# Six graph-attention layers on one core: exponentials of layer 0 in other slots, layer 1's projection tied to ScalarE's copies, and a new order for the last items

## The chip, the core and the metric

The kernel runs on one core of a Trainium2 chip. TensorE (PE, with its weight loads shown as PEld), VectorE (DVE), ScalarE (ACT), GpSimd (POOL) and SyncE (SP, which issues the DMAs) each work through a queue of their own in order, and wait for each other only through semaphores. The metric is device microseconds of one execution.

## The reference, cut to what matters

128 graphs of 128 nodes with 256 features pass through six attention layers. Layer 0 has eight heads, layer 1 one head of width 256, layers 2 to 5 one head of width 128.

```
layer 0:     q,k,v = x@W + b ; attn = softmax(mask(q k^T / sqrt(32))) per head
             x = layernorm(x + (attn@v)@Wo + bo)
layer 1:     attn = softmax(mask((x@Wq)(x@Wk)^T / 16)) ; x = layernorm(x + attn@(x@Wv)@Wo + bo)
layers 2..5: attn = softmax(mask((x@Wq+bq)(x@Wk+bk)^T / sqrt(128)))
             x = layernorm(x + (attn@x)@Wc^T)
```

## The kernel before, in words

**Groups and slots.** Two graphs make a group; there are 64 groups. The program is a list of slots, and every engine walks the same list, each with its own fixed order of work inside a slot. Five slots make a period. In a period the slots project, in order of time, layer 2, layer 1, layer 5, layer 4 and layer 3, each for another group (`item(i)` gives layer and group of slot i). An item is projected in its slot i, its softmax is done in slot i+1, and its context, residual and normalisation in slot i+2. Below, "the layer-2 slot" is the slot that projects layer 2.

**Layer 0 beside it.** Layer 0 of one group is spread over twelve slots (`due(i, lead)`: lead slots ahead of that group's layer 1). Its eight heads are four units j of two heads and two graphs. `score0` runs in the layer-2 slot (lead 6). DVE takes row maxima (`row_max0`, L820), ACT the four exponentials of each unit (`exp0`, L676), DVE the reciprocals of the sums (`reciprocal0`, L839), POOL multiplies the probabilities with them (`normalise_probs0`, L1035), and PE transposes the result (`transpose_probs0`, L506).

**Projection.** Numbers are split in a high and a low half: PE transposes x into `qk_bank` (L549, PSUM), ACT copies the bank to `xT_hi` (L698), DVE subtracts to get `xT_lo` (`split_lo`, L854, which reads `qk_bank`, in PSUM, and `xT_hi`, in SBUF), and PE multiplies (L442): for each output half and each of the two blocks of features the three products low weights by high x, high weights by high x, high weights by low x. It waits for `xT_lo` before the first of the twelve. For layer 1 ACT makes a second copy `xT` (L700), which the scores of layer 1 read, and `split_lo` waits for it.

**Normalisation.** DVE takes statistics, POOL finds the reciprocal deviation (L1028, L1030), DVE normalises (L913), POOL multiplies with gamma (`scale`, L1046) and adds beta (`shift`, L1054). POOL's order inside a slot is fixed: units 2 or 3 of layer 0 first, then the reciprocal deviation of item i-2, unit 1, the scale of item i-2, unit 0, the shift. In the first slots and the last ones DVE does scale and shift itself (`normalise_alone`, L933 and L938).

**The end.** After slot 315 no new group enters. The rest is layers 2 to 5 of the last groups: group 63 has layer 2 in slot 319, layer 3 in 323, layer 4 in 327 and layer 5 in 331; group 61 has layer 5 in 321, group 62 layer 4 in 322 and layer 5, moved by `MOVED`, in 328.

Of the kernel before, what the change touches and what calls it, by code (L numbers as in the profile page):

```python
# [13 lines left out]
P = 128  # L14
KD = D // P
# [42 lines left out]

LAST_FIRST = PERIOD * (GROUPS - 1)
MOVED = {LAST_FIRST + 11: LAST_FIRST + 13}


def item(i):

    if i in MOVED:
        return None
    for start, moved in MOVED.items():
        i = start if i == moved else i  # L70
    layer = 1 if i % PERIOD == 0 else LAYERS - i % PERIOD
    group = (i - STEP * (layer - 1)) // PERIOD
    return (layer, group) if 0 <= group < GROUPS else None
# [12 lines left out]
def due(i, lead):  # L86

    group, rest = divmod(i + lead, PERIOD)
    return group if rest == 0 and 0 <= group < GROUPS else None
# [59 lines left out]
def gnn_stack(nc: bass.Bass, x_in, xT_in, adj_in, w_in, rows_in, cols_in, eye_in, out):  # L149
# [12 lines left out]
    with ctx:  # L162
# [192 lines left out]
        def ring(i):  # L355
            return NTH[i] % RING
# [79 lines left out]
        def _(pe):  # L436
            def project(psum, hi, lo, parts):
                for n, (name, at) in enumerate(parts):
                    halves = ((w_lo, hi), (w_hi, hi), (w_hi, lo))
                    for kd in range(KD):  # L440
                        for w, xT_half in halves:
                            mm = pe.matmul(psum[:, n * G * N:(n + 1) * G * N], split(w, name, kd, at, at + P),  # L442
                                           flat(xT_half[:, kd]), start=kd == 0 and w is w_lo,
                                           stop=kd == KD - 1 and xT_half is lo)
                return mm
# [106 lines left out]

            def project_qk(i):
                layer, group = item(i)
                parts = [("scores1", 0), ("scores1", P)] if layer == 1 else [(f"wqT{layer}", 0), (f"wkT{layer}", 0)]
                pe.wait_ge(xT_lo_ready, after(i))
                project(qk_bank, xT_hi[:, ring(i)], xT_lo[:, ring(i)], parts).then_inc(qk_in_psum, 1)

            def project_v(i, g):
                layer, group = item(i)  # L560
# [38 lines left out]
            for i in SLOTS:  # L599
                if i == 0:  # L600
                    pe.wait_ge(w1_lo_ready, 2)
                if i in LATER_SLOTS:
                    pe.wait_ge(later_lo_ready, LATER_SLOTS.index(i) + 1)
                if item(i - 1) and not scored_early(i - 1):
                    score(i - 1)
                if item(i - 1) and late_values(i - 1):
                    project_v(i - 1, 1)
                if (group := due(i, 6)) is not None:
                    score0(group)
                if (group := due(i, 4)) is not None:  # L610
                    transpose_probs0(group, 1)
                if (group := due(i, 8)) is not None:
                    project_q0(group)
                if (group := due(i, 7)) is not None:
                    project_k0(group)
                if item(i - 2):
                    context(i - 2)
                if item(i):
                    project_qk(i)
                if (group := due(i, 9)) is not None:  # L620
                    project_v0(group)
                if (group := due(i, 3)) is not None:
                    transpose_probs0(group, 3)
                if (group := due(i, 2)) is not None:
                    join_heads(group)
                if item(i - 1):
                    transpose_probs(i - 1)
                if item(i):
                    project_v(i, 0)
                if item(i) and scored_early(i):  # L630
                    score(i)
                if item(i) and not late_values(i):
                    project_v(i, 1)
                if (group := due(i, 5)) is not None:
                    transpose_probs0(group, 0)
                if (group := due(i, 4)) is not None:
                    transpose_probs0(group, 2)
                if (group := due(i, 3)) is not None:
                    heads0(group)
                if item(i + 1):  # L640
                    transpose_x(i + 1)
                if i == -6:
                    fuse_layer1()

        @block.scalar
        def _(act):
# [22 lines left out]
                                       bias=col("bk0", ft))  # L669
                m.then_inc(k0_ready, 1)  # L670

            def exp0(group, j):
                act.wait_ge(negmax0_ready, after_unit(group, j))
                for g in range(G):
                    for quad in range(QUADS):
                        e = act.activation(probs0[:, j, g, quad], scores0[:, j, g, quad], ACT.Exp, scale=-1.0,  # L676
                                           bias=negmax0[:, j, g, quad:quad + 1],
                                           accum_out=total0[:, j, g, quad:quad + 1])
                e.then_inc(exp0_ready, 1)

            def move_probs0T(group, j):
                act.wait_ge(probs0T_in_psum, after_unit(group, j))
# [58 lines left out]
            for i in SLOTS:  # L741
                if item(i):
                    split_hi(i)
                if item(i - 1) and item(i - 1)[0] != 1 and not late_values(i - 1):
                    move_v(i - 1)
                if (group := due(i, 4)) is not None:
                    move_probs0T(group, 0)
                if (group := due(i, 3)) is not None:
                    move_probs0T(group, 2)
                if (group := due(i, 2)) is not None:  # L750
                    move_headsT(group)
                if (group := due(i, 12)) is not None:
                    split_x0T(group)
                if i == FIRST:
                    for name in FIRST_WEIGHTS:
                        split_first(name)
                if item(i - 1):
                    softmax(i - 1)
                if item(i - 1) and late_values(i - 1):
                    move_v(i - 1)  # L760
                if (group := due(i, 6)) is not None:
                    exp0(group, 0)
                if (group := due(i, 5)) is not None:
                    exp0(group, 1)
                if (group := due(i, 4)) is not None:
                    move_probs0T(group, 1)
                    exp0(group, 3)
                if (group := due(i, 8)) is not None:
                    move_q0(group)
                if (group := due(i, 7)) is not None:  # L770
                    move_k0(group)
                if item(i):
                    move_qk(i)
                if item(i - 1):
                    move_probsT(i - 1)
                if (group := due(i, 5)) is not None:
                    exp0(group, 2)
                if (group := due(i, 3)) is not None:
                    move_probs0T(group, 3)
                if i == -5:  # L780
                    split_fused(0)
                    split_fused(1)
                if i + LATER_LEAD in LATER_SLOTS:
                    split_later(LATER_SLOTS.index(i + LATER_LEAD))

        @block.vector
        def _(dve):
# [58 lines left out]

            def split_lo(i):
                layer, group = item(i)
                if layer == 1:

                    dve.wait_ge(xT_ready, group + 1)
                else:
                    dve.wait_ge(xT_hi_ready, after(i))
                dve.tensor_tensor(flat3(xT_lo[:, ring(i)]), qk_bank[:, :], flat3(xT_hi[:, ring(i)]).bitcast(F32),  # L854
                                  ALU.subtract).then_inc(xT_lo_ready, 1)

            def row_max(i):
# [96 lines left out]
            for i in SLOTS:  # L954
                if item(i - 1):
                    row_max(i - 1)
                if item(i):
                    split_lo(i)
                if (group := due(i, 1)) is not None:
                    finish_or_normalise(("group", group))  # L960
# [4 lines left out]
                if (group := due(i, 5)) is not None:  # L965
                    reciprocal0(group, 0)
                    row_max0(group, 2)
                if (group := due(i, 4)) is not None:
                    reciprocal0(group, 2)
                if item(i - 1) and item(i - 1)[0] == 1:  # L970
                    move_v1(i - 1)
                if item(i - 2):
# [1 line left out]
                    statistics(("item", i - 2))  # L974
                if item(i - 1):
                    reciprocal_total(i - 1)
                if (group := due(i, 6)) is not None:
                    row_max0(group, 1)
                if (group := due(i, 5)) is not None:
                    reciprocal0(group, 1)  # L980
                    row_max0(group, 3)
                if (group := due(i, 9)) is not None:
                    move_v0(group)
                if (group := due(i, 4)) is not None:
                    find_valid(group)
                    reciprocal0(group, 3)
                if (group := due(i, 8)) is not None:
                    make_mask(group)
                if item(i - 2):
# [141 lines left out]
```

## Time and profile before

| | |
|---|---|
| time, median of 3 runs | 2371.49 us (2371.39 to 2374.79) |
| profiled execution, its own time | 2373.87 us |
| its span, first to last instruction | 2372.1 us |
| PE busy | 2259.9 us, 95% |
| PEld busy | 2136.2 us, 90% |
| DVE busy | 1783.3 us, 75% |
| ACT busy | 1620.0 us, 68% |
| POOL busy | 1794.9 us, 76% |
| DMA, mean | 29 GB/s |

Each row of the busy table is the time in which the engine ran an instruction, and its share of the span. PE is the engine that is nearly full. The share says nothing on which of its short waits can be taken away; that is read from the waits and from one period's instructions.

### The profile page before, as it was taken

The numbers are of one execution on the slowest core, as the hardware profiler recorded it, in microseconds if no ns is written. First come the engines' busy times: TensorE is split into PE (matmuls) and PEld (weight loads), VectorE is DVE, ScalarE is ACT, GpSimd is POOL, SyncE is SP. The second block draws the span as 40 slices with busy tenths as digits, with TensorE's granted clock in tenths as the row PEclk, the third lists the DMA queues.
The fourth block names the chain that finished last, engine by engine and source line by source line (L and its number), as shares of the span: only waits on it lengthen the run. The fifth ranks groups of instructions, "written<-read, shape, count | busy, mean of one in ns | idle before, by whom it ended". The sixth has DMA issues, their size and how long they took to land.

```text
span 2372.1 us, 59576 instructions
## 1 busy us (share of the span) xinstructions
PE 2259.9 (95%) x20624; PEld 2136.2 (90%) x20624; DVE 1783.3 (75%) x7734; ACT 1620.0 (68%) x5515; POOL 1794.9 (76%) x2399
## 2 busy tenths in 40 slices
PE   6899999999999999999999999999999999999985
PEld 5799999999999999999999999999999999999974
DVE  4777777777877877877877877877777777777864
ACT  5667767767767767767767767766766766767742
POOL 3368878878878878878878878878878878878751
PEclk9999999999999999999999999999999999999998
DMA  4000000100110000010010000000010010000000
GB/s 154 20 23 24 30 28 24 30 28 25 29 28 25 29 28 26 28 28 26 28 28 27 27 28 28 26 28 28 26 28 28 26 28 28 26 29 17 15 10 14
DMA packets 38747, 68.78 MB, mean 29 GB/s; under 512 B 4400, under 2 KB 12848, under 8 KB 37936
## 3 DMA queue, kind: packets, MB, share of 16 engines
q1 hardware_dynamic: 38448, 64.97, 9.0%
q8 instruction: 166, 2.72, 0.5%
q14 instruction: 133, 1.09, 0.2%
HBM read 48.18 MB, written 16.78 MB: 27 GB/s over the span
## 4 chain that ended last, share of the span: by engine, by line
PE 80%; DVE 9%; ACT 7%; issue 2%; POOL 1%; DMA 0%; POOLq 0%; SPq 0%; DVEq 0%
PE value_bank L450 17%; PE qk_bank L442 16%; PE context_bank L595 9%; PE unit_bank L450 7%; PE unit_bank L442 7%; PE qk_bank L549 7%; PE score_bank L579 5%; ACT probs L676 5%; PE unit_bank L506 4%; PE unit_bank L518 3%; DVE scores L820 2%; PE score_bank L576 2%; PE score_bank L586 2%; DVE xT_lo L854 2%; DVE scores L860 1%
## 5 line engine op out<-in xcount | busy, mean ns | idle before, releaser
L1046 POOL TENSOR_TENSOR x<-y,rows 128x512 f32<-128x512 f32 x305 | 392.0, 1285 | 188.9 <-DVE y L913 188.9
L698 ACT CAST xT_hi<-qk_bank 128x512 fp32r<-128x512 f32 x320 | 187.7, 587 | 399.8 <-PE qk_bank L549 399.6
L676 ACT ACTIVATE probs<-scores,negmax 128x128 f32<-128x128 f32 x1024 | 399.1, 393 | 88.6 <-DVE negmax L820 88.6
L913 DVE TENSOR_SCALAR y<-y,mv,rstd 128x256 f32<-128x256 f32 x730 | 304.2, 459 | 191.6 <-POOL rstd L1030 191.3
L442 PE MATMUL qk_bank<-xT_hi,w_lo 128*128 128x256 f32 x1280 | 411.5, 321 | 21.6 <-DVE xT_lo L854 21.3
L1054 POOL TENSOR_TENSOR x<-x,rows 128x512 f32<-128x512 f32 x305 | 393.8, 1291 | 19.2
L450 PE MATMUL value_bank<-w_lo,xT_hi 128*128 128x256 f32 x1280 | 394.4, 308 | 0.0
L442 PE MATMUL qk_bank<-xT_lo,w_hi 128*128 128x256 f32 x1280 | 363.5, 284 | 0.0
L442 PE MATMUL qk_bank<-xT_hi,w_hi 128*128 128x256 f32 x1280 | 362.1, 283 | 0.0
L450 PE MATMUL value_bank<-w_hi,xT_lo 128*128 128x256 f32 x1280 | 361.8, 283 | 0.0
L450 PE MATMUL value_bank<-w_hi,xT_hi 128*128 128x256 f32 x1280 | 361.0, 282 | 0.0
L894 DVE SCALAR_TENSOR_TENSOR y<-context_bank,rtotal,x 128x256 f32<-128x256 f32 x640 | 279.1, 478 | 97.4 <-PE context_bank L595 97.2
L1035 POOL TENSOR_TENSOR probs<-probs,rtotal 128x256 f32<-128x256 f32 x512 | 307.4, 622 | 48.3 <-DVE rtotal L839 48.3
L595 PE MATMUL context_bank<-v,probsT 128*128 128x256 f32 x1280 | 335.8, 385 | 1.4 <-ACT probsT L727 1.4
L442 PEld LDWEIGHTS qk_bank<-xT_hi,w_lo 128*128 128x128 f32 x1280 | 243.9, 191 | 67.5 <-DVE xT_lo L854 59.4
L1030 POOL TENSOR_TENSOR rstd<-var_eps,minus_half 128x2 f32<-128x2 f32 x384 | 273.0, 711 | 32.0
L860 DVE CUSTOM_DVE_ANT_0 scores<-score_bank,mask 128x128 f32<-128x128 f32 x640 | 160.8, 289 | 179.6 <-PE score_bank L579 159.6
L902 DVE BATCH_NORM_STATS2 bn<-y 128x6 f32<-128x256 f32 x768 | 285.2, 414 | 0.0
L721 ACT ACTIVATE probs<-scores,negmax 128x128 f32<-128x128 f32 x640 | 253.7, 402 | 27.0 <-DVE negmax L860 26.9
L549 PE MATMUL qk_bank<-eye,x 128*128 128x128 f32 x1280 | 198.7, 278 | 59.0 <-ACT kT L710 48.7
L442 PEld LDWEIGHTS qk_bank<-xT_hi,w_hi 128*128 128x128 f32 x1280 | 244.4, 191 | 4.6
L450 PEld LDWEIGHTS value_bank<-w_hi,xT_hi 128*128 128x128 f32 x1280 | 244.4, 191 | 0.0
(93 smaller groups left out, 6503.3 us busy)
## 6 DMA issues: line engine op xcount, KB each, us to landing
x0T<-xT_in SPq DMA_DIRECT2D x64, 256.0 KB, 3.0
x<-x_in SPq DMA_DIRECT2D x64, 256.0 KB, 3.0
out<-x_out SPq DMA_DIRECT2D x64, 256.0 KB, 2.3
adj<-adj_in SPq DMA_DIRECT2D x64, 128.0 KB, 2.2
late_weights<-w_in SPq DMA_DIRECT2D x2, 1024.0 KB, 7.1
rows<-rows_in SPq DMA_DIRECT2D x1, 1792.0 KB, 11.7
probs0T<-w_in SPq DMA_DIRECT2D x4, 256.0 KB, 4.2
x<-w_in SPq DMA_DIRECT2D x1, 1024.0 KB, 13.2
```

The costliest lines, as they stand in the source:

```text
L442: mm = pe.matmul(psum[:, n * G * N:(n + 1) * G * N], split(w, name, kd, at, at + P), flat(xT_half[:, kd]), start=kd == 0 and w is w_lo, st ...
L450: mm = pe.matmul(psum[:, g * D:(g + 1) * D], xT_half[:, kd, g], split(w, name, kd), start=kd == 0 and w is w_lo, stop=kd == KD - 1 and xT_ ...
L549: t = pe.transpose(qk_bank[:, (kd * G + g) * N:(kd * G + g + 1) * N], x[:, group % HELD, g, kd * P:(kd + 1) * P], eye[:, :])
L595: mm = pe.matmul(context_bank[:, g * D:(g + 1) * D], probsT[:, ring(i), g], v[:, ring(i), g], start=True, stop=True)
L676: e = act.activation(probs0[:, j, g, quad], scores0[:, j, g, quad], ACT.Exp, scale=-1.0, bias=negmax0[:, j, g, quad:quad + 1], accum_out=t ...
L894: dve.scalar_tensor_tensor(y[:, r, g], psum[:, g * D:(g + 1) * D], factor[:, g:g + 1], kept[:, g], ALU.mult, ALU.add).then_inc(y_ready, 1)
L902: last = note(dve.bn_stats(bn[:, r, g], y[:, r, g]))
L913: m = dve.tensor_scalar(y[:, r, g], y[:, r, g], mv[:, r, g, 0:1], rstd[:, r, g:g + 1], ALU.subtract, ALU.mult)
L1030: pool.tensor_tensor(rstd[:, r], var_eps[:, r], minus_half[:, :], ALU.pow).then_inc(rstd_ready, 1)
L1035: m = pool.tensor_tensor(probs0[:, j, g], probs0[:, j, g], rtotal0[:, j, g].unsqueeze(2).to_broadcast([P, QUADS, N]), ALU.mult)
L1046: pool.tensor_tensor(result(norm), y[:, NORM_AT[norm] % YS], row_of_each(f"gamma{layer}"), ALU.mult).then_inc(zg_ready, 1)
L1054: pool.tensor_tensor(result(norm), result(norm), row_of_each(f"beta{layer}"), ALU.add).then_inc(x_ready, 1)
```

## The change

1. `exp0` can do one graph alone. Unit 0's exponentials are done graph 0 before and graph 1 behind the copies of q and k in the layer-2 slot. Unit 2 moves from the end of the layer-1 slot to the middle of the layer-5 slot, and unit 3 from there to that slot's end. DVE's row maxima of unit 3 and the reciprocals of units 2 and 3 move with them.
2. Layer 1 gets a projection of its own: PE waits for `xT`, does the eight products with `xT_hi`, then waits for `xT_lo` and does the other four. Since the products overwrite `qk_bank`, `split_lo` of layer 1 now reads `xT` in SBUF instead of `qk_bank`.
3. The last items: group 63 is in slots 319, 322, 325 and 328; group 61's layer 5 stays in 321, group 62's layer 4 goes to 324 and its layer 5 to 327. For 321, 324 and 327 DVE's `split_lo` moves behind the statistics of item i-2 (for 321 at the end of the slot before).

```diff
-MOVED = {LAST_FIRST + 11: LAST_FIRST + 13}
+MOVED = {LAST_FIRST + 7: LAST_FIRST + 9, LAST_FIRST + 8: LAST_FIRST + 7, LAST_FIRST + 11: LAST_FIRST + 12,
+         LAST_FIRST + 12: LAST_FIRST + 10, LAST_FIRST + 16: LAST_FIRST + 13}
+PLACED = {slot: regular for regular, slot in MOVED.items()}
+FILL_IN = [LAST_FIRST + 6, LAST_FIRST + 9, LAST_FIRST + 12]
 ...
+            def project_fused(i):
 ...
+                pe.wait_ge(xT_ready, group + 1)
+                for n in range(KD):
+                    for kd in range(KD):
+                        for w in (w_lo, w_hi):
+                            pe.matmul(qk_bank[...n...], split(w, "scores1", kd, n * P, n * P + P), flat(hi[:, kd]), ...)
+                pe.wait_ge(xT_lo_ready, after(i))
+                for n in range(KD):
+                    for kd in range(KD):
+                        mm = pe.matmul(qk_bank[...n...], split(w_hi, "scores1", kd, n * P, n * P + P), flat(lo[:, kd]), ...)
+                mm.then_inc(qk_in_psum, 1)
 ...
-            def exp0(group, j):
+            def exp0(group, j, graphs=range(G)):
 ...
                 if (group := due(i, 6)) is not None:
-                    exp0(group, 0)
+                    exp0(group, 0, [0])
                 if (group := due(i, 4)) is not None:
                     move_probs0T(group, 1)
-                    exp0(group, 3)
+                    exp0(group, 2)
 ...                                   # behind move_qk(i) and move_probsT(i - 1)
-                if (group := due(i, 5)) is not None:
-                    exp0(group, 2)
+                if (group := due(i, 6)) is not None:
+                    exp0(group, 0, [1])
+                if (group := due(i, 4)) is not None:
+                    exp0(group, 3)
 ...                                   # split_lo
+                source = qk_bank[:, :]
                 if layer == 1:
                     dve.wait_ge(xT_ready, group + 1)
+                    source = flat3(xT[:, :])
-                dve.tensor_tensor(flat3(xT_lo[:, ring(i)]), qk_bank[:, :], flat3(xT_hi[:, ring(i)]).bitcast(F32),
+                dve.tensor_tensor(flat3(xT_lo[:, ring(i)]), source, flat3(xT_hi[:, ring(i)]).bitcast(F32),
 ...                                   # DVE's slots
-                if item(i):
+                if item(i) and not fills_in(i):
                     split_lo(i)
-                if (group := due(i, 4)) is not None:
-                    reciprocal0(group, 2)
+                if (group := due(i, 3)) is not None:
+                    reciprocal0(group, 3)
 ...                                   # behind reciprocal_total(i - 1)
+                if i + 1 == FILL_IN[0]:
+                    split_lo(i + 1)
+                if i in FILL_IN[1:]:
+                    split_lo(i)
                 if (group := due(i, 5)) is not None:
                     reciprocal0(group, 1)
+                if (group := due(i, 4)) is not None:
+                    reciprocal0(group, 2)
                     row_max0(group, 3)
```

## Rows read from the trace of the kernel before

**Rows 1.** Waits between 150 and 2250: who waits, for whom, us in total, times, longest
```profile
PE qk_bank L549 <- ACT kT L710: 43.0, 59, 0.7
PEld qk_bank L549 <- POOL x L1054: 53.1, 59, 0.9
POOL probs L1035 <- DVE rtotal L839: 10.0, 59, 0.2
```

**Rows 2.** Chain of waits near the last full period: start, duration, what
```profile
2253.74 1.15 POOL probs L1035 x2
...
2254.94 0.66 PE unit_bank L506 x4
```

**Rows 3.** Timeline of PEld and PE, one period; in brackets idle before and releaser
```profile
1205.45 0.20 PEld L549 LDWEIGHTS qk_bank<-eye,x 128*128 128x128 f32 x2 [0.91 <-POOL x L1054]
1214.30 0.19 PEld L442 LDWEIGHTS qk_bank<-xT_hi,w_lo 128*128 128x128 f32 x1 [0.30 <-DVE xT_lo L854]
1223.92 0.60 PE L506 MATMUL unit_bank<-eye,probs 128*128 128x128 f32 x4
```

**Rows 4.** Timeline of ACT, layer-2 slot of the same period
```profile
1202.96 0.40 ACT L676 ACTIVATE probs<-scores,negmax 128x128 f32<-128x128 f32 x1 [1.26 <-DVE negmax L820]
...
1204.52 0.46 ACT L708 ACTIVATE qT<-qk_bank,cols 128x256 f32<-128x256 f32 x1
```

**Rows 5.** Timeline of POOL, same period
```profile
1203.53 1.30 POOL L1054 TENSOR_TENSOR x<-x,rows 128x512 f32<-128x512 f32 x1
...
1206.65 1.28 POOL L1046 TENSOR_TENSOR x<-y,rows 128x512 f32<-128x512 f32 x1 [0.69 <-DVE y L913]
1208.10 1.19 POOL L1035 TENSOR_TENSOR probs<-probs,rtotal 128x256 f32<-128x256 f32 x2 [0.17 <-DVE rtotal L839]
...
1216.82 1.18 POOL L1035 TENSOR_TENSOR probs<-probs,rtotal 128x256 f32<-128x256 f32 x2
...
1222.43 1.18 POOL L1035 TENSOR_TENSOR probs<-probs,rtotal 128x256 f32<-128x256 f32 x2
```

**Rows 6.** Timeline of DVE, layer-1 slot and start of the layer-5 slot
```profile
1207.02 0.08 DVE L860 DVE_READ_ACCUMULATOR2_ANT negmax<- 128x1 f32 x1
1207.25 0.69 DVE L854 TENSOR_TENSOR xT_lo<-qk_bank,xT_hi 128x512 fp32r<-128x512 f32 x1
1207.86 0.17 DVE L839 RECIPROCAL rtotal<-total 128x4 f32<-128x4 f32 x1
...
1211.64 1.31 DVE L913 TENSOR_SCALAR y<-y,mv,rstd 128x256 f32<-128x256 f32 x2 [0.19 <-POOL rstd L1030]
1213.14 0.29 DVE L860 CUSTOM_DVE_ANT_0 scores<-score_bank,mask 128x128 f32<-128x128 f32 x1 [0.18 <-PE score_bank L576]
```

**Rows 7.** Timeline of POOL, at the start of the kernel
```profile
5.23 1.27 POOL L1008 TENSOR_TENSOR x0T_lo<-x0T,x0T_hi 128x512 fp32r<-128x512 f32 x1 [4.41 <-ACT x0T_hi L654]
```

**Rows 8.** Timeline of DVE, at the start of the kernel
```profile
5.79 1.26 DVE L796 TENSOR_TENSOR w_lo<-probs0T,w_hi 128x512 fp32r<-128x512 f32 x1
...
6.97 1.36 DVE L796 TENSOR_TENSOR w_lo<-probs0T,w_hi 128x512 fp32r<-128x512 f32 x2
```

**Rows 9.** Chain of waits behind slot 318: start, duration, what
```profile
2295.90 1.71 PE qk_bank L442 x12
...
2305.98 2.94 PE qk_bank L442 x12
...
2313.09 1.71 PE qk_bank L442 x12
...
2319.31 1.71 PE qk_bank L442 x12
...
2330.49 0.52 POOL var_eps L1028
...
2335.36 2.93 PE qk_bank L442 x12
...
2356.61 2.93 PE qk_bank L442 x12
```

More of the change, by code:

```diff
@@ L61, with fills_in @@
 LAST_FIRST = PERIOD * (GROUPS - 1)
-MOVED = {LAST_FIRST + 11: LAST_FIRST + 13}
+MOVED = {LAST_FIRST + 7: LAST_FIRST + 9, LAST_FIRST + 8: LAST_FIRST + 7, LAST_FIRST + 11: LAST_FIRST + 12,
+         LAST_FIRST + 12: LAST_FIRST + 10, LAST_FIRST + 16: LAST_FIRST + 13}
+PLACED = {slot: regular for regular, slot in MOVED.items()}
+FILL_IN = [LAST_FIRST + 6, LAST_FIRST + 9, LAST_FIRST + 12]
+def fills_in(i):
+    return i in FILL_IN
 def item(i):
-    if i in MOVED:
+    if i in MOVED and i not in PLACED:
         return None
-    for start, moved in MOVED.items():
-        i = start if i == moved else i
+    i = PLACED.get(i, i)
     layer = 1 if i % PERIOD == 0 else LAYERS - i % PERIOD
@@ L554, in project_qk @@
                 layer, group = item(i)
-                parts = [("scores1", 0), ("scores1", P)] if layer == 1 else [(f"wqT{layer}", 0), (f"wkT{layer}", 0)]
                 pe.wait_ge(xT_lo_ready, after(i))
-                project(qk_bank, xT_hi[:, ring(i)], xT_lo[:, ring(i)], parts).then_inc(qk_in_psum, 1)
+                project(qk_bank, xT_hi[:, ring(i)], xT_lo[:, ring(i)],
+                        [(f"wqT{layer}", 0), (f"wkT{layer}", 0)]).then_inc(qk_in_psum, 1)
+            def project_fused(i):
+                layer, group = item(i)
+                hi, lo = xT_hi[:, ring(i)], xT_lo[:, ring(i)]
+                pe.wait_ge(xT_ready, group + 1)
+                for n in range(KD):
+                    for kd in range(KD):
+                        for w in (w_lo, w_hi):
+                            pe.matmul(qk_bank[:, n * G * N:(n + 1) * G * N], split(w, "scores1", kd, n * P, n * P + P),
+                                      flat(hi[:, kd]), start=n == 0 and kd == 0 and w is w_lo, stop=False)
+                pe.wait_ge(xT_lo_ready, after(i))
+                for n in range(KD):
+                    for kd in range(KD):
+                        mm = pe.matmul(qk_bank[:, n * G * N:(n + 1) * G * N], split(w_hi, "scores1", kd, n * P, n * P + P),
+                                       flat(lo[:, kd]), start=False, stop=n == KD - 1 and kd == KD - 1)
+                mm.then_inc(qk_in_psum, 1)
             def project_v(i, g):
@@ L617, in _ @@
                     context(i - 2)
-                if item(i):
+                if item(i) and item(i)[0] == 1:
+                    project_fused(i)
+                elif item(i):
                     project_qk(i)
@@ L670, in move_k0 @@
                 m.then_inc(k0_ready, 1)
-            def exp0(group, j):
+            def exp0(group, j, graphs=range(G)):
                 act.wait_ge(negmax0_ready, after_unit(group, j))
-                for g in range(G):
+                for g in graphs:
                     for quad in range(QUADS):
@@ L678, in exp0 @@
                                            accum_out=total0[:, j, g, quad:quad + 1])
-                e.then_inc(exp0_ready, 1)
+                if g == G - 1:
+                    e.then_inc(exp0_ready, 1)
             def move_probs0T(group, j):
@@ L956, in _ @@
                     row_max(i - 1)
-                if item(i):
+                if item(i) and not fills_in(i):
                     split_lo(i)
@@ L985, in _ @@
                     find_valid(group)
-                    reciprocal0(group, 3)
                 if (group := due(i, 8)) is not None:
```

## The prediction

> **What bounds the kernel now.** I read the busy table first: PE is at 95%, so only its remaining waits can be won. The waits of the even stretch (150 to 2250, 59 periods) name two. Before layer 1's transposes PE waits 43.0/59 = 0.73 us per period for ACT's copy of k; the weight load ahead of them waits 53.1/59 = 0.90, and there the view names POOL's shift, not ACT [rows 1]. So two things end close together, and removing one uncovers the other. The other stall is in front of layer 5's projection, 0.30 per period [rows 3].
>
> Then I read one period engine by engine, since a second engine may be as tight as PE. It is POOL. From unit 0's multiplication to unit 3's its work hangs together: it waits 0.17 per period (10.0/59) for the reciprocal of unit 0 [rows 1, 5], and from then on runs nearly through, each piece behind the last or behind a DVE step that POOL itself releases. Unit 3 is done at 1222.43 + 1.18 = 1223.61 and PE transposes it at 1223.92 [rows 3, 5]. Near the end, where PE has less to do, the chain shows how fast that can go: POOL done at 2253.74 + 1.15 = 2254.89, PE at 2254.94 [rows 2]. So 0.05 is needed and 0.31 there: POOL's chain has only 0.26 us of slack in each period. A second branch leaves it: DVE's normalisation at 1211.64 (to 1212.95) waits for POOL, and the row maximum behind it starts at 1213.14, having waited 0.18 for PE [rows 6]. That one leads through `split_lo` to layer 5's projection. Its slack is 0.19.
>
> **Part 1, the exponentials.** Unit 0's four start at 0.39 us intervals (1202.96 to 1204.52) [rows 4]; two of them leave the path to the copies, 0.78. The copies cannot start before the projection has ended, about 1203.85, so they come some 0.65 earlier. PE's transposes could then start at about 1204.80, but POOL's shift ends at 1203.53 + 1.30 = 1204.83 [rows 5], and takes over: the load goes from 1205.45 [rows 3] to about 1204.87, a gain of 0.58 at this place, not 0.73. The two deferred exponentials run behind the copies and are done by 1205.65, when the transposes are; they delay nothing.
>
> Unit 2's exponentials take the place of unit 3's in the layer-5 slot, so the copies there come as before. Its reciprocal now stands behind the statistics on DVE; adding up that engine's steps behind 1213.14 I estimate it done near 1216.3. POOL took unit 2 up at 1216.82 [rows 5] and, without its wait of 0.17, would at 1216.65, so this costs nothing. Cover: 0.3 us; if it is gone, POOL stops with `normalise_probs0(2)` at its head, and the reciprocal deviation and the scale behind it. Unit 3's exponentials go behind the copy of layer 1's probabilities, where ACT has only PE's next transposes to wait for. No DMA is moved, and SP's queue is passed nowhere.
>
> **Part 2, layer 1's projection.** PE may start two thirds of it without `xT_lo`, so the subtraction (0.69 [rows 6]) leaves PE's path there; twelve products before and after. PE is not what is short at this place, though. The price lies in the new operand: `split_lo` of layer 1 now has both inputs in SBUF.
>
> The trace has such an instruction, same form, once beside POOL: `split_weight` starts at 5.79 while POOL's `x0T_lo` runs from 5.23 to 6.50, and takes 1.26; the next two take 1.36 together, 0.68 each [rows 7, 8]. So it stood still until 1.26 - 0.68 = 0.58 after its start, 6.37, that is until 0.13 before POOL's end. In the period, the row maximum ends at 1207.02 + 0.08 and `xT`, for which the old one waited until 1207.25, is ready half a microsecond earlier, so `split_lo` starts near 1207.05. POOL's scale runs from 1206.65 to 1207.93 [rows 5], and always will: it is released by the normalisation that stands just ahead of that row maximum. The old form, with one input in PSUM, ran there in 0.69 [rows 6].
>
> The step: stand still to 1207.93 - 0.13 = 1207.80; the reciprocal of unit 0 follows 0.61 after (as 1207.25 to 1207.86), POOL 0.24 after that (1207.86 to 1208.10): 1208.65 instead of 1208.10, so +0.55 for the whole of POOL's chain. Against the slacks: unit 3's transposes come 0.55 - 0.26 = 0.29 later, layer 5's projection 0.55 - 0.19 = 0.36 later. The larger one counts, and 0.36 on PE also covers the 0.29. PE's gain of 0.58 lies ahead of both places and is lost in waiting there. With 59 periods in the even stretch and one more at its ends: 60 x 0.36 = +21.6; I take +21.
>
> Bounds: if the new operand costs nothing, POOL loses its wait of 0.17, the two branches can come 0.17 + 0.26 = 0.43 and 0.17 + 0.19 = 0.36 earlier; the smaller, less 0.02 that DVE needs between two instructions, is all that PE can win: -0.34, 60 times -20. If DVE stands still to POOL's very end, +0.13 more: 0.49, +29.
>
> The Trainium skill (SBUF — State Buffer, section "Who interferes with whom") says that a VectorE instruction with two SBUF inputs contends with a GpSimd instruction that reads SBUF, and that the loser blocks for the whole instruction. On the pair at 5.23 and 5.79 the first holds; the second is 0.13 too much, and by it the sum would be the +29.
>
> **Part 3, the end.** Group 63's projections start at 2295.90 (layer 2), 2319.31, 2335.36, 2356.61 (layer 5) [rows 9]; steps of 23.4, 16.05 and 21.25, and 15.5 to the span's end. New, step by step. Layer 2 to 3: only group 61's layer 5 lies between, and its normalisation precedes, as group 62's did in the step of 16.05; I take 16. Layer 3 to 4: the fill-in's `split_lo` comes behind the statistics, which end 11.1 after the projection (2319.31 to 2330.49 less a step), then 0.7, and PE must run the fill-in's projection before the transposes of group 63: 7.1 from projection to projection (2305.98 to 2313.09), in all 18.9. Layer 4 to 5: the same, and the fill-in's transposes wait for the result that the fill-in before it has just given, some 2 more: 21. Last layer: 15.5, up to 1 more for the item ahead of it. Sum 71.9 against 76.2: -4.5. Of these steps the projections of 2.93 stand against 1.71 elsewhere [rows 9]; if denser work keeps them at 1.71, three times 1.2 more are won: -8. If each new wait adds one: 0.
>
> **Start.** The first two groups have little beside layer 0, so unit 3's later exponentials lie open, at most one unit (1.56) each; against it stand layer 1's earlier projection starts (0.69 each) and copies (0.78 each). I take 0, from -2 to +2.
>
> **Sum.** +21 - 4.5 + 0 = +16.5 on the profiled execution's 2373.87: 2390.4. That execution was 2.4 above the median; on the median, 2388.
>
> **Rivals.** *The subtraction passes beside POOL.* Then only gains are left: -20 - 4.5, 2347. For it: one pair of rows at the start is thin, and scheduling may shift. Against it: it is the same operation on as many columns, and POOL's scale reads SBUF too. It decides at a delay of unit 0's multiplication of 0.19, from which on layer 5's projection is late; with the end's gain counted in, at 0.27 (0.19 + 4.5/60).
>
> *It stands still, but POOL's chain has slack that the rows hide*, since spans on POOL are rough: the even part then comes out near 0 and the end's gain stays, 2367 (2358 to 2374). For it: half a microsecond is to be swallowed. Against it: the chain with 0.05 to PE [rows 2].
>
> *Unit 2's reciprocal comes late as well*, because DVE stands behind exponentials in ACT's queue: POOL's head is blocked; every 0.1 beyond the cover of 0.3 is 6 us; 0.5 beyond gives 2418. Against it: POOL itself is 0.55 later, which doubles the cover.
>
> **How the numbers follow.** Forecast 0.70, with a range of its own of 2376 to 2404 (even part 17 to 29, end -8 to 0, start -2 to +2). No stop 0.15 (2338 to 2356). Hidden slack 0.11. Late reciprocal 0.04. The range for 8 in 10, 2357 to 2404, holds the forecast, nearly all of the hidden slack, and leaves out the two others. A difference of under 0.2% (4.7 us) is what a measurement here can't tell from none. Faster: 0.15 and half of 0.11, 0.20. The same: the rest of that and the forecast's low edge, 0.08. Slower: 0.72.
>
> **What would show it.** Right: DVE's layer-1 `xT_lo` at about 1.4 instead of 0.69 in 60 places; the transposes of layer 1 waiting for POOL's shift and no longer for k; new PE waits for POOL's probabilities of unit 1, and a longer one before layer 5's projection; a period of 36.0 instead of 35.6. Wrong: layer-1 `xT_lo` near 0.69 beside POOL's scale, and a period of 35.3; or 60 rows of 1.4 with a period that stays. The end: 72 us from group 63's layer-2 projection instead of 76.

## The result and the profile after

The changed kernel takes 2395.44 us in the median of four runs (2386.0 to 2397.34), the kernel before 2372.53 (2371.39 to 2374.79): ratio 1.0087, 95% interval 1.006 to 1.0115. It is slower, as forecast; 2388 was predicted. The profiled execution is the fastest of the four, 2386.0 us with a span of 2384.2, so a comparison of the two traces has to explain 12.1 us of span and not 23. The spans of two further profiles of the changed kernel, described below, are 15.0 and 16.5 above that of the kernel before.

Three stretches hold it. The same instruction of every group, `score0`, cuts them out: group 5's starts the even part (the first one with all layers running) and group 63's ends it, 58 periods later. Kernel before, timeline of PE:

```profile
169.36 1.17 PE L495 MATMUL unit_bank<-k0T,q0T 32*128 32x128 f32 x32
...
2231.46 1.17 PE L495 MATMUL unit_bank<-k0T,q0T 32*128 32x128 f32 x32
```

Changed kernel, the same two:

```profile
167.61 1.17 PE L502 MATMUL unit_bank<-k0T,q0T 32*128 32x128 f32 x32
...
2249.15 1.17 PE L502 MATMUL unit_bank<-k0T,q0T 32*128 32x128 f32 x32
```

The start is 169.36 before and 167.61 now: -1.75. The period is (2231.46 - 169.36)/58 = 35.553 and (2249.15 - 167.61)/58 = 35.889: +0.336, 58 times +19.5. The end, from group 63's `score0` to the end of the span, is 2372.1 - 2231.46 = 140.64 and 2384.2 - 2249.15 = 135.05: -5.6. Together +12.1.

The three stretches are not equally clean. The clock that TensorE was granted is 1.00 of full speed (2.4 GHz) from 170 to 2230 us in both executions. Outside it is a mean of the two levels, 2.4 and 1.2 GHz, and differs: from 70 to 110 and from 110 to 170 us it is 0.91 and 0.97 before and 1.00 and 1.00 now, and in the end 0.91 before and 0.94 now. So +0.336 per period can be read as the change's own, but -1.75 and -5.6 may be the clock's in part.

**The subtraction.** First its forms, with smallest, median and largest duration in ns, over the whole changed kernel:

```profile
L885 DVE TENSOR_TENSOR xT_lo<-qk_bank,xT_hi x256: 658/685/691, 65.4 to 2367.8; 128x512 fp32r<-128x512 f32 x128
L885 DVE TENSOR_TENSOR xT_lo<-xT,xT_hi x64: 686/1570/1577, 41.1 to 2291.2; 128x512 fp32r<-128x512 f32 x64
```

The instruction with two inputs in SBUF takes 686 ns where nothing hinders it, no more than the one with the bank, and 1570 in the median. One period of DVE's timeline, the counterpart of [rows 6]; times lie 8.23 us behind those of the period shown there, going by the start of POOL's scale (1206.65 there, 1214.88 here):

```profile
1214.07 0.74 DVE L944 TENSOR_SCALAR y<-y,mv,rstd 128x256 f32<-128x256 f32 x2 [0.37 <-POOL rstd L1066]
1215.14 1.57 DVE L885 TENSOR_TENSOR xT_lo<-xT,xT_hi 128x512 fp32r<-128x512 f32 x1
1216.64 0.16 DVE L869 RECIPROCAL rtotal<-total 128x4 f32<-128x4 f32 x1
```

And POOL's, the counterpart of [rows 5]:

```profile
1214.88 1.28 POOL L1082 TENSOR_TENSOR x<-y,rows 128x512 f32<-128x512 f32 x1 [0.69 <-DVE y L944]
1216.88 1.18 POOL L1071 TENSOR_TENSOR probs<-probs,rtotal 128x256 f32<-128x256 f32 x2 [0.72 <-DVE rtotal L869]
...
1231.21 1.18 POOL L1071 TENSOR_TENSOR probs<-probs,rtotal 128x256 f32<-128x256 f32 x2
```

DVE comes to the subtraction at 1215.14, 0.26 behind the start of POOL's scale, and ends at 1216.71; less its own 0.69 it ran from 1216.02, 0.14 before POOL's end at 1216.16. The reciprocal follows at 1216.64, and POOL takes up unit 0 at 1216.88. The forecast of 1208.65, moved by 8.23, is 1216.88 too. No semaphore makes this wait, and no list of waits shows it: the profile counts it as work of DVE, whose busy time is 1837.6 us instead of 1783.3.

**What waits now.** Waits between 150 and 2250 of the changed kernel, PE, PEld and POOL:

```profile
PE unit_bank L513 <- POOL probs L1071: 41.4, 58, 0.7
PEld unit_bank L513 <- POOL probs L1071: 52.4, 58, 0.9
PEld qk_bank L556 <- POOL x L1090: 19.0, 58, 0.3
PEld qk_bank L580 <- DVE xT_lo L885: 13.2, 58, 0.2
POOL probs L1071 <- DVE rtotal L869: 41.5, 58, 0.7
```

The wait of 0.73 for ACT's k has gone from PE's list, and one as long for POOL's probabilities stands in its place. POOL's own wait for the reciprocal grew from 0.17 to 0.72. The weight loads of the changed kernel show where in the period that happens (the counterpart of [rows 3]):

```profile
1213.11 0.42 PEld L556 LDWEIGHTS qk_bank<-eye,x 128*128 128x128 f32 x4 [0.33 <-POOL x L1090]
1216.77 0.54 PEld L580 LDWEIGHTS qk_bank<-xT_lo,w_hi 128*128 128x128 f32 x4 [0.23 <-DVE xT_lo L885]
1221.63 0.42 PEld L513 LDWEIGHTS unit_bank<-eye,probs 128*128 128x128 f32 x4 [0.91 <-POOL probs L1071]
```

Layer 1's transposes do come earlier: the load is at 1213.11, which is 1204.88 in the period of before, against 1205.45 there. Eight and a half microseconds on, at the transposes of unit 1, PE gives it back.

### The profile page after: what moved, and what is told of

Read it like the earlier page. It is cut to its first block, busy times and chain, and to the rows that moved or that the text cites. A ratio compares the mean times of both kernels' runs of the same rounds, so it can differ in the third digit from the quotient of the medians.

```text
span 2384.2 us, 59576 instructions
## 1 busy us (share of the span) xinstructions
PE 2264.0 (95%) x20624; PEld 2137.2 (90%) x20624; DVE 1837.6 (77%) x7734; ACT 1630.4 (68%) x5515; POOL 1791.8 (75%) x2399
## 4 chain that ended last, share of the span: by engine, by line
PE 60%; POOL 22%; DVE 10%; issue 5%; ACT 2%; DMA 0%; POOLq 0%; SPq 0%; DVEq 0%
PE qk_bank L449 11%; PE value_bank L457 11%; PE unit_bank L449 7%; PE unit_bank L457 7%; PE context_bank L620 7%; POOL x L1090 7%; POOL probs L1071 6%; PE unit_bank L513 4%; POOL rstd L1066 4%; PE qk_bank L556 4%; PE score_bank L604 4%; POOL x L1082 3%; DVE y L944 3%; DVE xT_lo L885 3%; PE unit_bank L525 3%
## 5 line engine op out<-in xcount | busy, mean ns | idle before, releaser
L449 PE MATMUL qk_bank<-xT_hi,w_lo 128*128 128x256 f32 x1024 | 335.3, 327 | 13.1 <-DVE xT_lo L885 13.0
L449 PE MATMUL qk_bank<-xT_lo,w_hi 128*128 128x256 f32 x1024 | 289.7, 283 | 0.0
L449 PE MATMUL qk_bank<-xT_hi,w_hi 128*128 128x256 f32 x1024 | 288.4, 282 | 0.0
L457 PEld LDWEIGHTS value_bank<-w_lo,xT_hi 128*128 128x128 f32 x1280 | 242.2, 189 | 0.1
L457 PEld LDWEIGHTS value_bank<-w_hi,xT_lo 128*128 128x128 f32 x1280 | 241.2, 188 | 0.0
L620 PEld LDWEIGHTS context_bank<-v,probsT 128*128 128x128 f32 x1280 | 217.7, 189 | 25.4 <-ACT probsT L755 1.2
```

Source lines behind the costliest of these rows:

```text
L457: mm = pe.matmul(psum[:, g * D:(g + 1) * D], xT_half[:, kd, g], split(w, name, kd), start=kd == 0 and w is w_lo, stop=kd == KD - 1 and xT_ ...
L620: mm = pe.matmul(context_bank[:, g * D:(g + 1) * D], probsT[:, ring(i), g], v[:, ring(i), g], start=True, stop=True)
```

## The experiments

The theory under test: two inputs in SBUF make DVE stand still while POOL's scale reads SBUF, and POOL's chain, which has little slack, is late by that. Rivals: the later exponentials and reciprocals of part 1; the new order of products in part 2; a cost of the operand that has nothing to do with POOL.

**Without part 2.** Layer 1 goes back to the old projection, and the subtraction to the bank.

```diff
-                if item(i) and item(i)[0] == 1:
-                    project_fused(i)
-                elif item(i):
+                if item(i):
                     project_qk(i)
...
-                    source = flat3(xT[:, :])
```

> The changed kernel without part 2: layer 1 is projected as before, and its xT_lo is subtracted from the PSUM bank again. Theory (the operand in SBUF makes DVE stand still behind POOL's scale, and POOL's chain is late by that): layer-1 xT_lo 0.69 again instead of 1.57, the period 35.2 to 35.3 instead of 35.89, time about 2347. Rival (part 1's later reciprocals of units 2 and 3 block POOL): the period stays at 35.9, time 2385 or more.

Measured: 2351.08 us (2348.64 to 2351.5), ratio to before 0.991 (0.9895 to 0.9925): faster than both kernels. Period 35.156, start 174.22, end 136.0. All subtractions have their old length:

```profile
L864 DVE TENSOR_TENSOR xT_lo<-qk_bank,xT_hi x320: 658/686/693, 43.2 to 2332.9; 128x512 fp32r<-128x512 f32 x160
```

Part 1 as the cost is out: with it and without part 2 the period falls by 0.40. The prediction had 0.34 as the most that PE could win here; that bound was too low. A period from one profile is good to about 0.05: kernels below with the same even part have 35.156 and 35.186, or 35.553 and 35.511. The 4 us more than expected lie in the start, 174.2 against 169.4 before.

**Part 2 alone.** The kernel before with the fused projection and the operand in SBUF.

> The kernel before with part 2 alone. Theory: layer-1 xT_lo about 1.4 to 1.6, period 35.9, time 2372 + 20 = 2392. Rival (part 1 is what costs): period 35.55 or less, time 2372 or a little under, since PE waits less for xT_lo.

Measured: 2398.04 us (2397.66 to 2399.34), ratio 1.0111 (1.0096 to 1.0126). Period 35.959, start 169.75, end 140.5. Part 2 by itself costs 0.41 per period; the theory holds. The subtraction took 1.23 in the median and not 1.4 to 1.6: as with the operand alone, below, it comes later than in the changed kernel, counted from the start of POOL's scale, by 0.32.

**Part 3 alone.** `MOVED`, `item` and the places of `split_lo` in the last slots.

> The kernel before with part 3 alone. Both theories: the period stays at 35.55; from group 63's last score0 to the end 135 instead of 140.7 us, time about 2367. If the end's gain belongs to the other parts: 2372.

Measured: 2366.61 us (2365.98 to 2369.0, 10 runs), ratio 0.9981 (0.9972 to 0.9991). Period 35.511, end 136.2 instead of 140.6. The end's gain is part 3's own.

**The operand alone.** The kernel before in which one input of one instruction changes; PE waits for `xT_lo` as ever.

```diff
                 if layer == 1:
                     dve.wait_ge(xT_ready, group + 1)
+                    source = flat3(xT[:, :])
```

> The kernel before in which only layer 1's xT_lo reads xT in SBUF instead of the PSUM bank; PE's projection, the exponentials and the end as before. Theory: the operand alone gives xT_lo of 1.4 to 1.6 and a period of 35.9, time about 2392. Rival (the new order of products with its two waits costs, the operand does not): xT_lo 0.69, time 2372.

Measured: 2403.55 us (2402.92 to 2406.06), ratio 1.0135 (1.012 to 1.0151). Period 36.052: half a microsecond for one operand. DVE's timeline in this kernel:

```profile
1221.62 1.23 DVE L862 TENSOR_TENSOR xT_lo<-xT,xT_hi 128x512 fp32r<-128x512 f32 x1
```

POOL's beside it:

```profile
1221.03 1.28 POOL L1054 TENSOR_TENSOR x<-y,rows 128x512 f32<-128x512 f32 x1 [0.69 <-DVE y L921]
1223.02 1.19 POOL L1043 TENSOR_TENSOR probs<-probs,rtotal 128x256 f32<-128x256 f32 x2 [0.71 <-DVE rtotal L846]
```

The subtraction took 1.23 instead of the 1.4 to 1.6 expected, and the time was 11.5 us above the 2392. Counted from the start of POOL's scale it comes 0.33 later than in the changed kernel, since it waits for `xT` (ACT's copy ends at 1221.59), and so it takes 0.34 less: it ends when POOL lets it, not when it came. Against part 2 alone the period is 0.09 longer. So the new order of products gives 0.09 back; the rival that it costs is out.

**Part 1 alone.**

> The kernel before with part 1 alone. Theory: the period falls by the 0.40 that it fell by without part 2, to 35.16; the end stays at 140.6; the start is some 5 us longer, since the exponentials of units 2 and 3 lie open there (PE waits 12 us for POOL's probabilities in the first 150 us, instead of 2.4). Time about 2356. Rival (the gain of 0.40 belongs to the end's new order or needs it): 2372 or more.

Measured: 2353.68 us (2351.62 to 2358.17), ratio 0.993 (0.9915 to 0.9945). Period 35.204, start 172.4, end 142.2, at a granted clock of 0.88 there (0.91 before). Of the gain of 0.40 in the even part 0.35 needs nothing from the other parts; the rest is within what single profiles differ by. In the first 150 us PE waits (this kernel) for POOL's probabilities

```profile
PE unit_bank L512 <- POOL probs L1045: 12.7, 8, 2.3
```

against 2.4 us in the kernel before. That does not settle the start alone: in the changed kernel PE waits 13.9 us there for the same, and its start is not longer. There PE's wait for `xT_lo` in that stretch is 0.2 us, with 2.6 for `xT`, instead of 6.2, and the clock is 1.00 from 70 to 170 us instead of 0.96 and 0.97; how much each gives back is not shown.

**The changed kernel again**, unaltered: four runs, and later one more.

> The changed kernel once more, since one of its runs took 2386 and three took 2395 to 2397. Theory: the period is 35.89 in each and the end 135; the difference lies in the first 170 us, where PE runs at the lower clock in one and not in the other, so a run of 2395 shows group 5's score0 at about 176 instead of 167.6. Rival (the even part has two ways to settle): score0 of group 5 near 168 and a period of 36.04.

> The changed kernel once more, one look: either again near 2386 to 2390, with group 5's score0 near 167.5 and a period of 35.9, or near 2396; then the trace says whether the start, the period or the end is longer.

Measured: 2390.41 us (2389.1 to 2394.92), and 2390.39 in the later run. Two more profiles: spans 2387.1 and 2388.6, periods 35.908 and 35.888, starts 167.2 and 169.9, ends 137.2 in both instead of 135.05. So the period is the same in all three profiles to 0.02, and start and end differ by 2 to 3 us. They differ with the granted clock: the starts of 167.6 and 167.2 have 1.00 from 110 to 170 us and the one of 169.9 has 0.97; the end of 135.05 has 0.94 and the two of 137.2 have 0.92. A run of 2394 or more has not been profiled. The four such runs have a mean clock of 0.991 or 0.992, the five others 0.992 to 0.995, which leans the same way; which stretch is longer in them stays open, and neither expectation about them was met.

**Old places for the first groups.** Parts 1 and 3 without part 2; groups 0 to 2 keep the exponentials, row maxima and reciprocals where they were.

```diff
-                    exp0(group, 0, [0])
+                    exp0(group, 0, [0, 1] if group < EARLY else [0])
...
-                    exp0(group, 2)
+                    exp0(group, 3 if group < EARLY else 2)
```

> Parts 1 and 3 without part 2, and groups 0 to 2 keep the old places of their exponentials, row maxima and reciprocals. Theory: the start is as before (group 5's score0 at 169 instead of 174), the period 35.16, the end 136; time about 2346, faster than the one with part 1 in all groups (2351). Rival (the longer start comes from elsewhere): 2351.

Measured: 2349.89 us (2347.97 to 2350.69), ratio 0.991 (0.9895 to 0.9925). The start is 168.7 instead of 174.2, as expected, and PE's wait there falls to

```profile
PE unit_bank L514 <- POOL probs L1059: 4.3, 5, 2.0
```

but the end of this execution is 137.7 instead of 136.0, at a granted clock of 0.91 instead of 0.92, and the period 35.186 instead of 35.156. The medians lie 1.2 us apart and their ranges overlap: where the start's time lies is shown, that it shortens the kernel is not. It has the lowest median of the versions that do the whole computation.

**The reciprocal first.** The changed kernel; DVE takes unit 0's reciprocal ahead of the subtraction, so that POOL need not wait for it.

```diff
+                if (group := due(i, 5)) is not None:
+                    reciprocal0(group, 0)
                 if item(i) and not fills_in(i):
                     split_lo(i)
...
                 if (group := due(i, 5)) is not None:
-                    reciprocal0(group, 0)
                     row_max0(group, 2)
```

> The changed kernel, in which DVE takes unit 0's reciprocal ahead of layer 1's xT_lo instead of behind it; the operand stays in SBUF. Theory (POOL's chain is late because that reciprocal stands behind the stalled subtraction): the wait of POOL for it, 0.72 per period, goes; what is left is the subtraction's own time on the shared port, if it gets in first: period 35.6, time about 2380; if POOL gets in first, period 35.25, time 2358, with xT_lo longer than 1.57. Rival (the port alone costs, whatever stands behind it): period 35.89, time 2395.

Measured: 2386.2 us (2385.2 to 2388.36), ratio 1.0066 (1.0051 to 1.0081). Period 35.852, only 0.04 under that of the changed kernel, no more than single profiles differ by. My 35.6 was wrong. DVE in this kernel:

```profile
1216.50 0.17 DVE L869 RECIPROCAL rtotal<-total 128x4 f32<-128x4 f32 x1
1216.59 1.49 DVE L885 TENSOR_TENSOR xT_lo<-xT,xT_hi 128x512 fp32r<-128x512 f32 x1
```

POOL:

```profile
1216.24 1.28 POOL L1083 TENSOR_TENSOR x<-y,rows 128x512 f32<-128x512 f32 x1 [0.69 <-DVE y L944]
1217.48 1.64 POOL L1072 TENSOR_TENSOR probs<-probs,rtotal 128x256 f32<-128x256 f32 x2
```

POOL goes on to unit 0 at once, its wait is gone, and the two multiplications take 1.64 instead of 1.18: now POOL stands still for the subtraction. What follows on DVE is as late as before, the statistics of layer 3 too, and POOL waits for those instead:

```profile
POOL var_eps L1065 <- DVE mv L936: 103.0, 175, 2.7
```

In the changed kernel that wait is 84.7 us, 117 times. So the order of these two instructions on DVE is not what costs. The overlap itself does, whichever engine pays.

**POOL's scale cut short.** The changed kernel with all its waits and operands, where layer 4's scale multiplies one column of each graph. The kernel leaves out the other columns, so it does not compute the same result.

```diff
+                if layer == 4:
+                    pool.tensor_tensor(result(norm)[:, :, 0:1], y[:, NORM_AT[norm] % YS, :, 0:1],
+                                       rows[:, at:at + 1, 0:1].to_broadcast([P, G, 1]), ALU.mult).then_inc(zg_ready, 1)
+                    return
```

> The changed kernel, in which POOL's scale of layer 4, the one that runs when layer 1's xT_lo is due, multiplies one column per graph instead of 256; the rest of layer 4's multiplication with gamma is left out. Operand, order and waits are those of the changed kernel. Theory (the subtraction stands still because POOL reads SBUF at that time): layer-1 xT_lo takes about 0.7 instead of 1.57, POOL's unit 0 starts near where it did before the change less 0.2, period about 35.15, time about 2350. Rival (two inputs in SBUF cost DVE by themselves, or meet PE or ACT there): xT_lo stays near 1.57, and the period falls only by what POOL's shorter queue gives.

Measured: 2338.35 us (2334.68 to 2342.38). Period 35.01. The subtraction with two inputs in SBUF, all 64 of them:

```profile
L885 DVE TENSOR_TENSOR xT_lo<-xT,xT_hi x64: 685/690/693, 41.0 to 2238.3; 128x512 fp32r<-128x512 f32 x64
```

One period of it, DVE and POOL:

```profile
1223.68 0.69 DVE L885 TENSOR_TENSOR xT_lo<-xT,xT_hi 128x512 fp32r<-128x512 f32 x1
```

```profile
1223.42 0.19 POOL L1084 TENSOR_TENSOR x<-y,rows 128x2 f32<-128x2 f32 x1 [0.69 <-DVE y L944]
1224.53 1.18 POOL L1071 TENSOR_TENSOR probs<-probs,rtotal 128x256 f32<-128x256 f32 x2 [0.92 <-DVE rtotal L869]
```

The scale is over at 1223.61, before the subtraction starts. The same instruction, in the same program on PE and ACT, takes 690 ns instead of 1570 when POOL runs nothing beside it. That settles what it stands still for; whether POOL's reading of SBUF or its writing is what counts, no run here tells apart. The time says less: it is 12 us under the 2350 expected, since the short scale also relieves POOL's chain.

## Why the prediction was right

**The sign and the mechanism.** The step that carried the forecast, DVE standing still behind POOL's scale until shortly before its end, came out to a hundredth: release 0.14 before POOL's end against 0.13 predicted, and unit 0 on POOL 0.55 later, as predicted. Counted from the start of POOL's scale, DVE came to the subtraction 0.14 earlier than forecast, so it took 1.57 and not about 1.4, and still ended on time. The rule of the Trainium skill ("SBUF — State Buffer", section "Who interferes with whom"), that such an instruction contends with a GpSimd instruction that reads SBUF, held; that the loser blocks for the whole instruction is 0.14 too long here, and its +29 for the even part too much.

**The even part** was set at +21 (0.36 over 60 periods) and measured +19.5 (0.336 over 58). The branch that I let decide was the wrong one, so that 0.36 lies near 0.336 is in part luck. Layer 5's projection no longer waits for `xT_lo`: the 0.30 in front of it [rows 3] is gone, since PE already comes late from the transposes of unit 1. The prediction named new waits of PE at unit 1 as a sign, but the slack that PE had there is not in its sum, and it was the smallest of all. Kernel before, POOL and PE at unit 1:

```profile
1211.57 1.23 POOL L1035 TENSOR_TENSOR probs<-probs,rtotal 128x256 f32<-128x256 f32 x2
```

```profile
1212.94 0.60 PE L506 MATMUL unit_bank<-eye,probs 128*128 128x128 f32 x4
```

POOL is done at 1212.80, PE follows 0.14 later, and with the 0.05 that is needed [rows 2] 0.09 of slack is left. Changed kernel, POOL at unit 1 and PE at units 1 and 3:

```profile
1220.35 1.23 POOL L1071 TENSOR_TENSOR probs<-probs,rtotal 128x256 f32<-128x256 f32 x2
```

```profile
1221.64 0.65 PE L513 MATMUL unit_bank<-eye,probs 128*128 128x128 f32 x4 [0.72 <-POOL probs L1071]
...
1232.27 0.28 PE L449 MATMUL qk_bank<-xT_lo,w_hi 128*128 128x256 f32 x1
1232.45 0.66 PE L513 MATMUL unit_bank<-eye,probs 128*128 128x128 f32 x4
```

Unit 1's transposes come 0.47 later (1221.64 is 1213.41 in the period of before), as 0.55 - 0.09 gives; some 0.17 of it comes back where layer 5's projection waited before. The transposes of unit 3 then come 0.30 later (1232.45 is 1224.22, against 1223.92 in [rows 3]), where the prediction's smaller figure was 0.29. That is nearly all of the 0.336. Two ties of PE to POOL's chain are thus close to each other: the only wait that the profile lists is at unit 1, and at unit 3, which POOL ends at 1231.21 + 1.18 = 1232.39, PE's first product starts 0.18 after the one ahead of it instead of 0.12, so PE is held there by about 0.06 more.

**Part 1** gains what was said of it, 0.58 at layer 1's transposes, and in the changed kernel nothing comes of it. Between the changed kernel and part 2 alone lie 0.07 per period, hardly more than single profiles differ by. Without part 2, part 1 is worth 0.35 by itself and 0.40 together with part 3. POOL's wait of 0.17 for the reciprocal goes there (1.1 and 1.2 us are left between 150 and 2250, instead of 10.0); that the slack of the two branches accounts for the rest is not shown. The cover named for unit 2's reciprocal held: POOL's listed waits for reciprocals are 0.72 per period, 58 in all, and belong to unit 0.

**The start** was set at 0, from -2 to +2. The three profiles of the changed kernel (167.61, 167.2 and 169.9 against 169.36) show -2.1 to +0.5. That is in part luck: the clock, 1.00 from 70 to 110 us in all three against 0.91 before, stood in no term. Part 1 without part 2 adds 3 to 5 us there, and with the old places for the first groups that goes, as the prediction's open exponentials would have it.

**The end** was set at -4.5 (its own terms add up to 71.9 - 76.2 = -4.3) and measured -5.6 in this profile and -3.4 in the two others. The chain behind slot 318 of the changed kernel, the counterpart of [rows 9]:

```profile
2314.64 1.69 PE qk_bank L449 x12
...
2330.04 1.70 PE qk_bank L449 x12
...
2341.42 2.93 PE qk_bank L449 x12
2347.82 1.71 PE qk_bank L449 x12
2361.43 2.93 PE qk_bank L449 x12
2368.57 1.70 PE qk_bank L449 x12
```

(The lines left out are those of other engines and lines.) Group 63's layers are at 2314.64, 2330.04, 2347.82 and 2368.57: steps of 15.4, 17.8, 20.75 and 15.6 to the span's end, 69.6 against 71.9 predicted (16, 18.9, 21 and 15.5 to 16.5) and 76.2 before. The fill-ins' projections at 2341.42 and 2361.43 stand before group 63's transposes and run at 2.93; group 63's own run at 1.70 in this profile. In the two others the one of layer 3 takes 2.93 and 2.95, at a granted clock of 0.91 from 2320 to 2340 us instead of 1.00. So the end has its size in part from the clock; part 3 alone gave -4.4.

**What was short.** The sum for the profiled execution was +16.5; it came to +12.1 there, and to +15.0 and +16.5 in the two later profiles. For the median it was 2388, and the first four runs gave 2395. Later runs of the same kernel gave 2390.41 and 2390.39. These differences of up to 11 us between runs, which go roughly with the granted clock, were in no term. The range of 2376 to 2404 is not quite what its parts add up to on 2371.49, which is 2378 to 2402.

## What to carry to other kernels

Before an operand moves from PSUM to SBUF, look at what GpSimd runs at that moment, since the lists of waits will not show the price: a VectorE instruction of 0.69 us became one of 1.57, although the copy that it now reads was there anyway. A gain on the fullest engine counts only up to the next engine's slack; POOL, busy 76%, had 0.26 us per period before unit 3 and 0.09 before unit 1. And a change of three parts is best priced part by part: here two of them together give 2351 and the third takes it all back.

## What the runs showed of the hardware that was not expected

Standing still is mutual and moves with the order: with the reciprocal first, POOL's two multiplications took 1.64 instead of 1.18 and DVE's subtraction still 1.49. The period is about the same as when DVE alone waited (35.852 and 35.889). The engines thus wait for each other not only through semaphores: here DVE and POOL did so without one.
